# Work moved into TensorE's waits in a two-layer vision kernel, and a new order for its closing rounds

## Chip, cores and metric

The kernel runs on one core of a Trainium2 chip. The metric is the device time of one execution in microseconds, from the first instruction to the last. Five engines work in parallel, each through its own queue in order: TensorE (PE in the profile, its weight loads PEld), VectorE (DVE), ScalarE (ACT), GpSimd (POOL), and SyncE (SP), which issues the transfers. They wait for one another by semaphores.

## What is computed

The input is (2, 96, 256, 256) in float32, taken through two layers. Each layer is x + mixer(norm(x)), then t + FFN(norm(t)) for every pixel's 96 channels.

```python
# layer 0
x = x + window_attention(_ln_c(x))      # 8x8 windows, 12x12 keys (halo 2), 6 heads of 16, rel. positions
t = t + ffn(_ln_t(t), W1, b1, W2, b2)   # 96 -> 384 -> 96, relu, products in fp8 (5, 2), sums in fp16
# layer 1
x = x + cluster(_ln_c(x))               # features, 4 centres per head and fold, cosine, sigmoid, argmax,
                                        # aggregate to the centres, mix back, projection
t = t + ffn(_ln_t(t), ...)
```

In layer 1 the centres are means of the normalised pixels over quarters of a quadrant, so every similarity of a quadrant needs the whole quadrant, and the mix needs the sums over all similarities of the quadrant.

## The kernel before

The image is cut into N = 128 strips: 8 quadrants of 128x128 pixels, 16 strips of 8 rows each. A strip has 16 windows, handled as 8 tiles `p` of two. All stages of one step `n` of the pipeline are written into one in-order list for each engine. Step n does the attention of strip n; the normalisation, keys and queries of strip n+1 (`ahead`); the first FFN of strip n-1 (`b1`); the features and similarities of layer 1 for strip n-18 (`b`, LAG_B = 18); the mix of strip n-34 (`c1`, LAG_C = 34); the hidden part of the second FFN of strip n-35 (`c2`); and its output for n-36 (`c3`). So strips 35 to 127 have every stage. After strip 127 there are closing rounds, `drain`: 18 with features (`b`), 16 with only the mix and the second FFN, and two more.

The order is by hand. In `attend` TensorE goes for each tile through scores(p+1), inserted work, `flip(p, 0)` and `flip(p, 1)` (transposes of the shifted scores, L723 and L726, into the two banks `flipped`), `weigh(p-1)` (probabilities times values, L745 and L751), and more inserted work. ScalarE takes exponentials out of `flipped` (L1241, L1244), VectorE takes maxima (L1573) and subtracts them (L1577, L1581). scores(p+1) waits until VectorE has shifted tile p. The inserted work shares the PSUM banks: `work` (two banks), `fill`, which is the two banks of `flipped`, `misc`, and `pv`.

What the change touches, with the lines of the profile: `mean` (L607) of the next strip and its variances (L616, twelve small matmuls into `misc`); the first FFN's transposes `flip_z` (L917, copied to z8t by ScalarE at L1309), hidden tiles (L930), bias on VectorE (L1720), quantise on ScalarE (L1320), output (L940); `make_keys` (L643, stored at L1184); queries (L660, L663, stored at L1190); the second FFN's `flip_zc` (L999), hidden_c (L1009, copied at L1371, bias L1871, quantise L1377), output_c (L1017, copied at L1383, added at L1877 and L1881); `flip_sims` (L985, stored at L1360); `mix` (L992, added at L1836); `best_of`, the ranking (L1805 to L1824), and `gather` (L975). hidden(3) is the first of the second half and waits for the second z8t. In the closing rounds: feature transposes (L958, copied at L1342), features (L965), squares (L1349), comparison (L1775), sums (L1780), root steps (L1452 to L1476), z8c (L1864), cosine (L1796).

## Time and profile before

| | us |
|---|---|
| median of 3 runs | 8884.77 (8862.72 to 8898.8) |
| profiled execution | 8874.92, its span 8873.0 |
| busy in the span | PE 7728.7 (87%), PEld 6203.8 (70%), DVE 6895.1 (78%), ACT 4875.0 (55%), POOL 2496.1 (28%) |
| transfers | 501.76 MB, mean 57 GB/s |

A busy share is an average over strips and closing rounds, which have different limits. The last three of the 40 slices of the span (about 665 us) are closing rounds: there the granted clock of TensorE is 0.5 to 0.6 of full speed and no engine is full. "issue" as a releaser means that the profile shows nothing that the engine waited for.

### The profile page before, as it was taken

The numbers are of one execution on the slowest core, as the hardware profiler recorded it, in microseconds if no ns is written. First come the engines' busy times: TensorE is split into PE (matmuls) and PEld (weight loads), VectorE is DVE, ScalarE is ACT, GpSimd is POOL, SyncE is SP. The second block draws the span as 40 slices with busy tenths as digits, with TensorE's granted clock in tenths as the row PEclk, the third lists the DMA queues.
The fourth block names the chain that finished last, engine by engine and source line by source line (L and its number), as shares of the span: only waits on it lengthen the run. The fifth ranks groups of instructions, "written<-read, shape, count | busy, mean of one in ns | idle before, by whom it ended". The sixth has DMA issues, their size and how long they took to land.

```text
span 8873.0 us, 429305 instructions
## 1 busy us (share of the span) xinstructions
PE 7728.7 (87%) x172050; PEld 6203.8 (70%) x172050; DVE 6895.1 (78%) x22530; ACT 4875.0 (55%) x9750; POOL 2496.1 (28%) x4860
## 2 busy tenths in 40 slices
PE   6999999998999899988999889998998989997655
PEld 4777777777777777777777777776777777775433
DVE  3677777777888888888888778887888878887666
ACT  2444545545656565555656556555565556655445
POOL 1333333333332333333232322322333223322000
PEclk7899999999999999999999989999999999998556
DMA  2111111121222222222222212222222222221111
GB/s 58 41 43 43 45 45 50 51 52 50 64 59 64 57 62 58 61 61 57 62 59 62 57 54 62 59 62 58 61 58 63 57 56 64 61 62 50 59 55 60
DMA packets 193344, 501.76 MB, mean 57 GB/s; under 512 B 33508, under 2 KB 67108, under 8 KB 191468
## 3 DMA queue, kind: packets, MB, share of 16 engines
q1 hardware_dynamic: 191692, 476.75, 19.5%
q8 instruction: 1401, 22.95, 1.1%
q14 instruction: 251, 2.06, 0.1%
HBM read 228.84 MB, written 169.93 MB: 45 GB/s over the span
## 4 chain that ended last, share of the span: by engine, by line
PE 67%; DVE 15%; issue 8%; ACT 8%; DMA 1%; SPq 0%; ACTq 0%; DVEq 0%; POOL 0%; POOLq 0%
PE scores_x L701 11%; PE flipped L723 6%; PE bank L660 6%; PE pv L751 4%; DVE maxes L1573 4%; PE bank L663 3%; PE misc L616 3%; PE bank L965 3%; PE bank L671 3%; PE scores_x L643 3%; PE bank L607 3%; PE pv L745 3%; DVE shifted L1581 2%; PE bank L678 2%; PE flipped L992 2%
## 5 line engine op out<-in xcount | busy, mean ns | idle before, releaser
L2049 POOL TENSOR_TENSOR vrest<-vstage,vmask 96x384 f32<-96x384 f32 x512 | 437.2, 854 | 4643.4 <-ACT vstage L1202 4643.4
L1573 DVE TENSOR_REDUCE maxes<-scores_x 128x6 f32<-128x864 f32 x1024 | 1077.6, 1052 | 757.3 <-PE scores_x L701 754.0
L701 PE MATMUL scores_x<-keys,queries 64*64 64x144 f32 x24576 | 1060.7, 304 | 102.4 <-DVE shifted L1581 67.0
L701 PEld LDWEIGHTS scores_x<-keys,queries 64*64 64x64 f32 x24576 | 777.5, 140 | 337.5 <-issue 295.7
L663 PE MATMUL bank<-xn,wq 97*32 97x64 f32 x24576 | 919.9, 224 | 88.5 <-issue 86.7
L660 PE MATMUL bank<-xt,wq 97*32 97x64 f32 x24576 | 899.0, 224 | 88.3 <-issue 84.0
L1581 DVE TENSOR_TENSOR shifted<-scores_x,maxes 128x768 f32<-128x768 f32 x1024 | 970.1, 947 | 0.0
L660 PEld LDWEIGHTS bank<-xt,wq 97*32 97x32 f32 x24576 | 758.7, 112 | 268.9 <-issue 203.8
L723 PE MATMUL flipped<-ident,shifted 128*128 128x128 f32 x6144 | 891.6, 284 | 0.2 <-ACT vstage L1202 0.2
L663 PEld LDWEIGHTS bank<-xn,wq 97*32 97x32 f32 x24576 | 773.2, 110 | 108.7 <-issue 108.1
L1241 ACT ACTIVATE probs<-flipped 128x384 f32<-128x384 f32 x1024 | 498.7, 487 | 600.2 <-PE flipped L723 599.7
L1190 ACT ACTIVATE queries<-bank 128x512 f32<-128x512 f32 x768 | 456.2, 594 | 659.6 <-PE bank L663 658.9
L723 PEld LDWEIGHTS flipped<-ident,shifted 128*128 128x128 f32 x6144 | 741.0, 149 | 80.5 <-issue 48.2
L2062 POOL TENSOR_SCALAR xn<-x,mr 128x96 f32<-128x96 f32 x1024 | 689.9, 686 | 51.0 <-DVE mr L1476 33.1
L751 PE MATMUL pv<-vmain,probs 128*32 128x17 f32 x49152 | 633.6, 188 | 0.0
L1244 ACT ACTIVATE probs<-flipped 128x512 f32<-128x512 f32 x1024 | 612.2, 598 | 26.7 <-PE flipped L726 26.7
L751 PEld LDWEIGHTS pv<-vmain,probs 128*32 128x32 f32 x49152 | 624.2, 114 | 0.1
L2031 POOL COPY win_xn<-xn 97x144 f32<-97x144 f32 x2048 | 539.1, 310 | 0.0
L2022 POOL COPY xt<-xn 97x512 f32<-97x512 f32 x256 | 291.1, 1168 | 869.4 <-DVE xn L1541 755.7
L1371 ACT ACTIVATE h16c<-flipped 128x512 f16<-128x512 f32 x768 | 423.0, 593 | 181.0 <-PE flipped L1009 181.0
L1377 ACT ACTIVATE h8c<-h16c 128x512 fp8e5<-128x512 f16 x768 | 451.8, 627 | 17.7 <-DVE h16c L1871 13.5
L1314 ACT ACTIVATE h<-flipped 128x512 f16<-128x512 f32 x768 | 427.8, 595 | 48.3 <-PE flipped L930 39.1
(196 smaller groups left out, 17204.1 us busy)
## 6 DMA issues: line engine op xcount, KB each, us to landing
keys<-kst SPq DMA_DIRECT2D x768, 99.0 KB
x_in<-x_dram SPq DMA_DIRECT2D x130, 396.0 KB
xn_kept<-xn SPq DMA_DIRECT2D x128, 388.0 KB, 2.5
later<-xn_kept SPq DMA_DIRECT2D x128, 388.0 KB, 3.4
x_tok<-tok_dram SPq DMA_DIRECT2D x128, 384.0 KB, 3.1
x_kept<-x SPq DMA_DIRECT2D x128, 384.0 KB, 2.3
later<-x_kept SPq DMA_DIRECT2D x128, 384.0 KB, 3.7
out_dram<-later SPq DMA_DIRECT2D x128, 384.0 KB, 2.4
```

Of the source, the lines that this page charges most:

```text
L660: mm(dst[64 * e:64 * e + 32, :, :, j], wq[0:PROW, p * WS + j, 2 * g + e, :], xt[0:PROW, p, j, :, :], start=True, stop=True, skip_group_che ...
L663: last = mm(dst[64 * e + 32:64 * e + 64, :, j, :], wq[0:PROW, 2 * WS + j, 2 * g + e, :], rows[:, j], start=True, stop=True, skip_group_che ...
L701: last = mm(score[e][64 * j:64 * j + 64, g * NKEY:(g + 1) * NKEY], queries[64 * e:64 * e + 64, g, w, :], keys[64 * e:64 * e + 64, g, :, WS ...
L723: last = nc.tensor.transpose(flipped[:, e, g * 128:(g + 1) * 128], shifted[:, p % 2, e * NG + g, :], ident[:, :])
L751: last = mm(pv[tok_, at + i * VC:at + (i + 1) * VC], probs[:, p % 2, i, tok_], vmain[:, 2 * p + part // 2, i, :], start=False, stop=True, ...
L1190: run(queries[:, g, p:NW:2, :], work[i % 2][:, :].rearrange("p (w t) -> p w t", t=64), ACT.Copy).then_inc(q_stored.sem, 1)
L1241: run(probs[:, p % 2, 0:NG, :].rearrange("p i n -> p (i n)"), flipped[:, 0, 0:NG * 128], ACT.Exp).then_inc(exp_ready.sem, 1)
L1244: run(probs[:, p % 2, NG:NH + 1, :].rearrange("p i n -> p (i n)"), flipped[:, 1, :], ACT.Exp).then_inc(exp_ready.sem, 1)
L1573: V.tensor_reduce(maxes[:, p % 2, :, :], sc, AX.X, ALU.max).then_inc(max_ready.sem, 1)
L1581: V.tensor_tensor(shifted[:, p % 2, :, :].rearrange("p (e g) k -> p e g k", e=2), sc[:, :, :, 0:MAIN], maxes[:, p % 2, :, :, None].to_broa ...
L2031: last = P.tensor_copy(win_xn[:, w, :].rearrange("p (a b) -> p a b", b=KW), xn[0:PROW, :, WS * w:WS * w + KW])
L2062: last = P.tensor_scalar(xn2[:, t, 0:C], x2[:, t, :], mr[:, t, 0:1], mr[:, t, 1:2], ALU.subtract, ALU.mult)
```

## The change

In the strips with attention:
- TensorE: mean 1 goes from before the transposes of tile 0 to behind them. Variances 0 and 1 go from tile 3 to the end of tile 2, between hidden tiles 2 and 3 of the first FFN; only variance 2 stays in tile 3. For that, `flip_z` of the second half writes the second `fill` bank instead of `misc`, and hidden(3) waits for z8t. `make_keys` 0 and 1 go in front of the wait for the exponentials of tile 7 and hidden_c 4 and 5.
- ScalarE: in tile 4 the quantises 4 and 5 go in front of the copy of the similarities; keys 0 and 1 are stored before the hidden_c copies 4 and 5.
- VectorE: the ranking goes between the first and the second mix.

In the closing rounds:
- TensorE: similarities and features go in front of the transposes of the second FFN, whose six hidden tiles then follow in one run.
- VectorE: the two roots of a round (8 columns for the second FFN, 32 for the features) become one of 40. The ranking goes between hidden_c 2 and 3. It no longer adds the outputs.
- GpSimd adds the outputs in all closing rounds: two additions for each half.

```diff
@@ -317,7 +317,7 @@
         c_bn = signal("c_bn", 2, LAG_C + 1)
-        newton_z = signal("newton_z", 8, N)
+        newton_z = signal("newton_z", 8, N + LAG_B)
         rstd_z = signal("rstd_z", 1, LAG_C + 1)
@@ -608,8 +608,10 @@
             def variance(n, c, on=None):
-                if c == 0 and on and on.b1:
-                    pe.wait_ge(zt_ready.sem, zt_ready.at(n - 2, 2))
+                if c == 0 and on and on.b:
+                    pe.wait_ge(ft_ready.sem, ft_ready.at(n - 1, 2))
+                elif c == 0 and on and on.b1:
+                    pe.wait_ge(zt_ready.sem, zt_ready.at(n - 2, 1))
                 pe.wait_ge(squared.sem, squared.at(n, c + 1))
@@ -798,7 +800,6 @@
                         mean(n + 1, 0)
-                        mean(n + 1, 1)
                     if p == 1 and ahead:
@@ -808,8 +809,7 @@
                     if p == 3 and ahead:
-                        for c in range(3):
-                            variance(n + 1, c, on)
+                        variance(n + 1, 2, on)
                     if p == 4:
@@ -839,6 +839,8 @@
                     if p == 0:
+                        if ahead:
+                            mean(n + 1, 1)
                         if on.c3:
@@ -848,9 +850,13 @@
                     if p == 2 and b1:
-                        if on.b:
-                            pe.wait_ge(ft_ready.sem, ft_ready.at(n, 2))
+                        pe.wait_ge(exp_ready.sem, exp_ready.at(n, 6))
+                        pe.wait_ge(h_evac.sem, h_evac.at(n - 1, 2))
                         flip_z(n - 1, 1)
+                        hidden(n - 1, 2)
+                    if p == 2 and ahead:
+                        variance(n + 1, 0, on)
+                        variance(n + 1, 1, on)
                     if p == 3 and on.c2:
@@ -865,7 +871,8 @@
                         pe.wait_ge(exp_ready.sem, exp_ready.at(n, 2 * p + 2))
-                        hidden(n - 1, 2 * p - 2)
+                        if p != 2:
+                            hidden(n - 1, 2 * p - 2)
                         hidden(n - 1, 2 * p - 1)
@@ -873,13 +880,13 @@
                         output(n - 1, 1)
+                    if p == 7 and ahead:
+                        make_keys(n + 1, 0)
+                        make_keys(n + 1, 1)
                     if on.c2 and p in (5, 6, 7):
...
                         hidden_c(n, 2 * p - 9)
-                if ahead:
-                    make_keys(n + 1, 0)
-                    make_keys(n + 1, 1)
                 weigh(TILES - 1)
@@ -913,8 +920,9 @@
                 pe.sem_inc(gate, 1)
+                dst = fill[1] if u else misc
                 for j in range(4):
-                    last = mm(misc[0:C, j * 128:(j + 1) * 128], z8[:, 4 * u + j, :], ident8[:, :],
+                    last = mm(dst[0:C, j * 128:(j + 1) * 128], z8[:, 4 * u + j, :], ident8[:, :],
                               start=True, stop=True)
@@ -922,6 +930,8 @@
                     pe.wait_ge(zt_ready.sem, zt_ready.at(f, u + 1))
+                if i == 3:
+                    pe.wait_ge(zt_ready.sem, zt_ready.at(f, 2))
                 if i >= 2:
@@ -1026,6 +1036,7 @@
                     flip_z(n, 1)
+                    pe.wait_ge(zt_ready.sem, zt_ready.at(n, 2))
                     for i in range(2 * NK):
@@ -1045,26 +1056,22 @@
                     flip_features(n, 1, k % 2)
+                if on.c1:
+                    flip_sims(n, on)
                 if on.c2:
                     pe.wait_ge(mixed.sem, mixed.at(n, 0))
+                if on.b:
+                    features(n, 0)
+                    features(n, 1)
+                    pe.wait_ge(fsq_ready.sem, fsq_ready.at(n, 2))
+                    pe.wait_ge(dots_ready.sem, dots_ready.at(n, 2))
+                if on.c2:
                     flip_zc(n, 0)
...
                         pe.wait_ge(yc_evac.sem, yc_evac.at(n, 2))
-                    for i in range(NK):
+                    for i in range(2 * NK):
                         hidden_c(n, i)
-                if on.c1:
-                    flip_sims(n, on)
-                if on.b:
-                    pe.wait_ge(zct_ready.sem, zct_ready.at(n, 2))
-                    features(n, 0)
-                    features(n, 1)
-                if on.c2:
-                    for i in range(NK, 2 * NK):
-                        hidden_c(n, i)
-                if on.b:
-                    pe.wait_ge(fsq_ready.sem, fsq_ready.at(n, 2))
-                    pe.wait_ge(dots_ready.sem, dots_ready.at(n, 2))
                 if on.c1:
@@ -1271,13 +1278,17 @@
                     if p == 4:
+                        if b1:
+                            quantise(n - 1, 4)
+                            quantise(n - 1, 5)
                         if on.c1:
...
                         if b1:
-                            quantise(n - 1, 4)
-                            quantise(n - 1, 5)
                             output(n - 1, 0)
                             output(n - 1, 1)
+                    if p == 7 and ahead:
+                        store_keys(n + 1, 0)
+                        store_keys(n + 1, 1)
                     if on.c2 and p in (5, 6, 7):
@@ -1287,8 +1298,6 @@
                 if ahead:
-                    store_keys(n + 1, 0)
-                    store_keys(n + 1, 1)
                     store_queries(n + 1, 0)
@@ -1306,7 +1315,7 @@
                 act.sem_inc(gate, 1)
-                run(z8t[:, u, :], misc[0:C, :], ACT.Copy, saturate=False).then_inc(zt_ready.sem, 1)
+                run(z8t[:, u, :], (fill[1] if u else misc)[0:C, :], ACT.Copy, saturate=False).then_inc(zt_ready.sem, 1)
@@ -1395,25 +1404,22 @@
                     flip_features(n, 1)
-                if on.c2:
-                    store_zc(n, 0)
-                    store_zc(n, 1)
-                    for i in range(NK):
-                        hidden_c(n, i)
-                        if i >= 1:
-                            quantise_c(n, i - 1)
                 if on.c1:
...
                 if on.c2:
-                    for i in range(NK, 2 * NK):
-                        hidden_c(n, i)
-                        quantise_c(n, i - 1)
-                    quantise_c(n, 2 * NK - 1)
+                    store_zc(n, 0)
+                    store_zc(n, 1)
                 if on.b:
                     similarity(n)
+                if on.c2:
+                    for i in range(2 * NK):
+                        hidden_c(n, i)
+                        if i >= 1:
+                            quantise_c(n, i - 1)
+                    quantise_c(n, 2 * NK - 1)
@@ -1666,9 +1672,10 @@
                     mix(n, 0, par, fill)
-                    mix(n, 1, par, fill)
                 if on.b:
                     best_of(n)
+                if on.c1:
+                    mix(n, 1, par, fill)
                 residual(1)
@@ -1884,20 +1891,28 @@
                     stats_c(n, 1 - par)
-                    rsqrt_c(n)
-                    normalise_c(n, 1 - par)
-                if on.c3:
-                    output_c(n, 0, par)
-                    output_c(n, 1, par)
-                if on.c2:
-                    for i in range(NK):
-                        hidden_c(n, i)
                 if on.b:
...
                     squares_sum(n, 1)
+                    dve.wait_ge(c_bn.sem, c_bn.at(n, 2))
+                    V.tensor_scalar(rs_b_chain[0][:, 32:32 + TILES], mv_z[:, :, 1], 1e-5, None, ALU.add)
                     lengths(n)
+                    rsqrt(rs_b_chain, n, 128, 32 + TILES, newton_d, 0,
+                          [(0, TILES * E1, rs_b_chain[3][:, 0:32], newton_n),
+                           (32, TILES, rs_c_chain[3][:, :], rstd_z)])
+                elif on.c2:
+                    rsqrt_c(n)
+                if on.c2:
+                    normalise_c(n, 1 - par)
+                if on.b:
+                    cosine(n)
+                if on.c2:
+                    for i in range(NK):
+                        hidden_c(n, i)
+                if on.b:
+                    best_of(n)
                 if on.c2:
@@ -1905,9 +1920,6 @@
                 if on.b:
-                    lone_root(n)
-                    cosine(n)
-                    best_of(n)
                     add_gathered(n)
@@ -2087,6 +2099,17 @@
+            def output_c(n, u, par):
+                pool.wait_ge(yc_evac.sem, yc_evac.at(n, u + 1))
+                pool.sem_inc(gate, 1)
+                P.tensor_tensor(y16c[:, u, :, :], y16c[:, u, :, :],
+                                b2q[1][:, None, :].to_broadcast([128, 4, C]), ALU.add
+                                ).then_inc(yc_biased.sem, 1)
+                pool.wait_ge(yc_biased.sem, yc_biased.at(n, u + 1))
+                pool.sem_inc(gate, 1)
+                P.tensor_tensor(xc[par][:, 4 * u:4 * u + 4, :], xc[par][:, 4 * u:4 * u + 4, :],
+                                y16c[:, u, :, :], ALU.add).then_inc(xc_ready.sem, 1)
+
             def strip(n, on, column=0):
@@ -2117,6 +2140,10 @@
             normalise_stream(N - 1)
+            with pool.Fori(0, (LAG_C + 2) // 2) as s:
+                for par in range(2):
+                    for u in range(2):
+                        output_c(2 * s + (N + par), u, par)
```

## Rows read from the trace of the kernel before

**Rows 1.** Stretches, one strip and some closing rounds: length, busy PE, PEld, DVE, ACT, POOL, clock, DMA
```profile
5031.88:5095.15 63.27, 56.22 (x1346) 45.55 (x1343) 52.41 (x171) 37.50 (x76) 19.50 (x38) 1.00 0.22 61
...
8250.00:8500.00 250.00, 151.98 (x840) 103.87 (x840) 165.37 (x680) 115.10 (x220) 0.00 (x0) 0.55 0.18 58
```

**Rows 2.** What TensorE waited for, 4000 to 7000 us: total us, times, longest
```profile
PE flipped L940 <- ACT h L1320: 44.8, 46, 1.0
PE flipped L1017 <- ACT probs L1244: 36.9, 47, 1.0
PE bank L663 <- issue: 35.3, 48, 1.6
...
PE flipped L930 <- ACT z8t L1309: 29.1, 46, 0.6
PE flipped L1009 <- ACT probs L1244: 29.0, 46, 0.6
...
PE pv L975 <- DVE simw L1824: 20.5, 33, 1.0
```

**Rows 3.** Timeline of one strip, tiles 0 to 5: start, us, engine, line, operation
```profile
5037.82 1.35 PE L607 MATMUL bank<-x_in,mean_w 96*97 96x352 f32 x4
...
5053.99 2.04 PE L616 MATMUL misc<-mean_w,kst 96*88 96x1 f32 x24
...
5054.13 1.06 DVE L1573 TENSOR_REDUCE maxes<-scores_x 128x6 f32<-128x864 f32 x1 [0.31 <-PE scores_x L701]
...
5059.69 1.06 DVE L1573 TENSOR_REDUCE maxes<-scores_x 128x6 f32<-128x864 f32 x1 [0.21 <-PE scores_x L701]
...
5061.91 1.27 DVE L1720 TENSOR_SCALAR h<-h,b1q 128x512 f16<-128x512 f16 x2
...
5062.18 0.84 POOL L2049 TENSOR_TENSOR vrest<-vstage,vmask 96x384 f32<-96x384 f32 x1 [15.78 <-ACT vstage L1202]
...
5063.64 1.14 ACT L1320 ACTIVATE h<-h 128x512 fp8e5<-128x512 f16 x2
...
5064.92 0.67 PE L940 MATMUL flipped<-w2q,h 128*128 128x96 fp8e5 x12 [1.01 <-ACT h L1320]
```

**Rows 4.** Timeline, the end of that strip and of the next, by engine
```profile
5078.65 1.35 PE L643 MATMUL scores_x<-xn,wk 97*96 97x352 f32 x4
...
5090.72 0.55 DVE L1836 TENSOR_TENSOR later<-later,flipped 128x384 f32<-128x384 f32 x1 [2.91 <-PE flipped L992]
...
5094.21 0.29 DVE L1824 TENSOR_TENSOR simw<-winners,sims 128x128 f32<-128x128 f32 x1 [0.20 <-DVE winners L1819]
...
5094.19 0.59 ACT L1190 ACTIVATE queries<-bank 128x512 f32<-128x512 f32 x1
```

**Rows 5.** Timeline of one closing round with features
```profile
8330.38 0.88 PE L975 MATMUL pv<-later,simw 128*32 128x97 f32 x16 [6.62 <-DVE simw L1824]
...
8335.63 0.60 ACT L1342 ACTIVATE later<-misc 97x512 f32<-97x512 f32 x1 [0.77 <-PE misc L958]
...
8335.74 2.00 DVE L1864 TENSOR_SCALAR z8c<-later,mv_z,rz 128x96 fp8e5<-128x96 f32 x8 [0.24 <-DVE rz L1476]
...
8338.90 1.07 ACT L1371 ACTIVATE h16c<-flipped 128x512 f16<-128x512 f32 x2
...
8340.43 3.59 PE L965 MATMUL bank<-wfa,later 97*128 97x112 f32 x16
```

**Rows 6.** Timeline of one of the last closing rounds, without features
```profile
8641.22 1.38 DVE L1843 BATCH_NORM_STATS2 bn_z<-later 128x6 f32<-128x96 f32 x8
...
8645.44 2.01 DVE L1864 TENSOR_SCALAR z8c<-later,mv_z,rz 128x96 fp8e5<-128x96 f32 x8 [0.24 <-DVE rz L1476]
...
8651.56 0.37 ACT L1360 ACTIVATE simw_t<-misc 128x256 f32<-128x256 f32 x1
```

**Rows 7.** One line each, 3300 to 8000 us: duration in ns, minimum/median/maximum
```profile
L1471 DVE SCALAR_TENSOR_TENSOR rn<-rn x77: 157/192/850, 3320.9 to 7973.4; 128x44 f32<-128x44 f32 x73, 96x4 f32<-96x4 f32 x4
...
L2068 POOL TENSOR_TENSOR xn_half<-xn x73: 869/875/879, 3300.0 to 7953.5; 128x388 f32<-128x388 f32 x73
```

## The prediction

> **What bounds the kernel now.** I read, in this order, the busy time of stretches, the waits of TensorE, and the timeline of one strip and of the closing rounds. A strip in full swing lasts 63.27 us; TensorE is busy for 56.22 of them, VectorE for 52.41, ScalarE for 37.50, GpSimd for 19.50 [rows 1]. So TensorE sets the strip's length, but VectorE is only 4 us behind, and what TensorE gains in one place counts only if VectorE can follow there. In the closing rounds no engine is full: in 250 us TensorE is busy for 151.98 and VectorE for 165.37, at a granted clock of 0.55 [rows 1]. There the round is a chain of latencies through three engines.
>
> The waits of TensorE over 47 strips show where its missing time lies [rows 2]. Per wait: 44.8/46 = 0.97 us in front of the second FFN output for ScalarE's last quantise; 36.9/47 = 0.79 in front of the layer 1 output (L1017) for the exponentials of tile 0; 29.1/46 = 0.63 in front of hidden tile 3 for z8t; 29.0/46 = 0.63 in front of hidden_c 4 for the exponentials of tile 7; 20.5/33 = 0.62 before the gather, in two strips of three, so about 0.4 a strip. Sum: 3.4 us a strip. The "issue" stops inside the queries (35.3/48 = 0.74 us each for L663) have no releaser in this profile, and the change does not touch them.
>
> **The full strips, part by part.** None of the edits adds or removes an instruction here; each moves work into one of those waits.
>
> Mean of chunk 1. Four passes for two chunks take 1.35 us, so one chunk about 0.6 [rows 3]. It leaves the place before the first transpose of tile 0, the transpose and the exponentials start 0.6 earlier, and it fills most of the 0.79. Gain 0.6, if nothing later binds.
>
> Variances 0 and 1. All three cost 2.04 us [rows 3], two of them 1.3. They fill the 0.63 before hidden tile 3, but are longer than it: scores of tile 4 go out 1.3 - 0.63 = 0.7 later than they would. With the 0.6 of the mean taken off, they come where they were, within 0.1. Two thirds of the variances no longer stand in front of the transpose of tile 3, so TensorE is 1.3 earlier from there on. VectorE is not: its maxima of tile 4 start at 5054.13 after 0.31 idle, those of tile 5 at 5059.69 after only 0.21 idle [rows 3], so between them it can give back 0.2. Through tile 5 VectorE decides, and TensorE's 1.3 us is so far a lead without effect.
>
> Quantise before the copy of the similarities. VectorE biases hidden tiles 4 and 5 from 5061.91 to 5063.18, where the second is held up by a GpSimd product (5062.18 to 5063.02) [rows 3]. ScalarE now quantises them from 5063.64 to 5064.78, and the second output starts at 5064.92 [rows 3]. With the copy moved behind, and ScalarE's exponentials earlier by TensorE's lead, the first quantise can start right behind the first bias (about 5062.4 to 5062.6) and the second ends at 5063.7 to 5063.9. The output starts at 5064.0: gain 0.9. This is where the lead of the two edits above and this one are cashed, 0.9 of 0.6 + 0.63 + 0.97 = 2.2; the rest goes to VectorE's pace.
>
> Keys 0 and 1. The two chunks (1.35 us with the drain of the last one [rows 4]) go in front of the wait for tile 7's exponentials and fill its 0.63. ScalarE stores them before the hidden_c copies instead of after, which leaves the length of its queue as it is. Gain 0.6.
>
> Ranking before the second mix. VectorE stood idle for 2.91 us until the second mix was ready, and only then ranked, from about 5091.2 to 5094.5 [rows 4]. Ranking is 3.3 us; placed into the idle time it ends 2.9 us earlier and the gather's wait goes. What is late next is the last copy of queries on ScalarE, ending at 5094.78 [rows 4], 0.9 us after TensorE's last query and needed by the next scores: the gather (0.54) hides only part of it. Gain 0.25. The second mix and the residual come after the ranking, still before TensorE's end.
>
> Sum: 0.9 + 0.6 + 0.25 = 1.75 a strip. I take 0.2 off because the "issue" stops sit in the stretch that now starts earlier and may grow: 1.55. The bounds are 0.5 (only the keys) and 3.4 (every wait closed). Such strips are those with all stages, 35 to 127: 93, so 144 us; bounds 46 and 316.
>
> The 34 earlier strips with a first FFN have no output_c and no hidden_c, so there the mean and the keys win nothing. Only the variances' 0.63 is left, against scores of tile 4 being 0.7 later for VectorE. I take 0.2 x 34 = 7 us, bounds -20 and +21.
>
> **Closing rounds with features (18).** One lasts 25.0 us. Now: gather at 8330.38, statistics, their own root, z8c at 8335.74 (5.4 later), the first hidden copy at 8338.90, the features between the hidden tiles at 8340.43 for 3.59, mix, then a second root (eight steps, about 1.8 us), cosine, exponential and the ranking (3.3), and the gather [rows 5]. After: the root waits for the features. Both feature transposes are copied at 8335.63 + 0.60, 5.85 after the gather [rows 5]; similarities 0.45, features 3.6, the squares 0.7, the comparison 0.2, the sums 1.0, the two small steps 0.4, the one root 2.1: z8c starts at 14.3 instead of 5.4. From there, without the 3.59 of features in the middle: hidden copy at 18.1 (3.16 as now, plus the similarity's 0.5), third bias at 20.8, ranking until 24.1, and only then biases 3 to 5. The last quantise ends near 27.0, against the gather at 24.9. The next round's second output waits for it (27.1 to 28.0), and its transposes follow. They now start 2.65 after the gather; 28.05 - 2.65 = 25.4. So the round is 0.4 longer: the second root (1.8) and the ranking come off the end, and the wait for the features is put in front. 18 x 0.4 = +7 us. The single steps have half a microsecond of doubt each, 1.5 a round: bounds -20 and +34.
>
> **Rounds without features (16, and the last ones).** The similarity copy (0.37, at 8651.56 among the hidden copies [rows 6]) leaves ScalarE's chain: -0.4. The output adds leave VectorE, where they stood in the shadow of the z8ct copies and cost nothing; GpSimd has four of them. No row has a 16-bit add on GpSimd; the nearest is a 32-bit sum of 388 elements, 875 ns [rows 7]. So they last about 4 x 0.9 = 3.6, roughly from 8642.3 to 8646.4 in the round of rows 6, over the root between the statistics (8641.22) and z8c (8645.44) [rows 6]. This is the cover that is missing: a root step of VectorE that overlaps a GpSimd product takes up to 850 ns instead of a median of 192 [rows 7], and the bias of [rows 3] took 1.27 for two for the same reason. If all steps in that span give way, z8c is 2.1 later; if GpSimd gives way, nothing. I take 1.2. In sum +0.8 x 17 = +14 us, bounds -7 and +29. The store of the outputs starts 2 to 3 us earlier, but only the odd round waits for it.
>
> The Trainium skill, "SBUF — State Buffer", section "SBUF: two separate sides", says that VectorE and GpSimd share a port pair under an exclusive lock held for a whole instruction, which a VectorE operation with two SBUF inputs needs. Row and rule agree on the kind of the wait; by the rule alone each two-input step meets a GpSimd add and the upper bound of +29 would hold. In the rounds with features the adds fall on the statistics, which have one input, and by row and rule cost nothing.
>
> **Sum.** -144 - 7 + 7 + 14 = -130 us. Against the profiled execution's own 8874.9 that gives 8745; the median of the runs is 8884.8, 10 above it, and I predict 8755 for the median.
>
> **Rivals.** *The gain is given back.* VectorE, 4 us behind TensorE [rows 1], keeps the pace past tile 5 as well, or the "issue" stops grow by what the keys gain. For it: 0.21 idle before tile 5 [rows 3]. Against it: VectorE is idle 2.91 at the end. A strip then gains 0.7: -65 - 0 + 21, near 8840.
> *All waits close.* VectorE follows since its own held-up operations shift away from GpSimd's. A strip gains 2.6, 93 x 2.6 = 242, the closings 0: near 8640. Against it is the same 0.21.
> *Slower.* The 1.3 us of variances in front of hidden tile 3 delay the scores of tile 4, and VectorE, which waits for those scores already (0.31 [rows 3]), is 0.7 later in each of 127 strips. It decides if scores 4 end later than now and VectorE is the bound from there to the end of the strip: +89, less 34 (0.37 in 93 strips) that the end of the strip would still give, so 8940. Against it: TensorE, not VectorE, has the longer busy time.
> *The port.* The strips gain as forecast, the closings cost their upper bounds, +34 + 29 instead of +21: near 8797. The lock that the page on SBUF describes would give this case.
>
> **How the numbers follow.** Forecast 0.52 (8755, its own range 8700 to 8800), given back 0.17, all waits close 0.13, slower 0.08, the port 0.10. For 8 in 10 the range reaches into the second and third: 8655 to 8850. What a measurement can tell from no change is 0.5%, 44 us. Faster: the forecast, all waits close, the port, and half of given back, which is 0.52 + 0.13 + 0.10 + 0.09 = 0.84, less 0.04 for a forecast that fails by its lower bounds: 0.80. Same 0.12, slower 0.08.
>
> **What the next profile would show.** Right: a strip of 61.5 to 62; no wait of L1017 over 0.3; no wait of hidden tile 3 for z8t; the second output's wait at 0.5 or less; no wait of hidden_c for the exponentials; the gather's wait gone and a short one of the scores for the last queries; maxima of tile 5 with no idle time before them. In the closings one root of 40 columns, rounds near 25.4, then 15 to 16.5 with root steps of over 0.5 us beside GpSimd's adds. Wrong: scores 4 later than 22 us after scores 0 with VectorE idle before its maxima; stops inside the queries well over 1.5 us a strip; or closing rounds over 27 us.

## The result, and the profile after

The changed kernel takes 8495.31 us in the median of 4 runs (8466.25 to 8505.01), beside 8887.02 (8862.72 to 8898.8) for the kernel before on the same chip: ratio 0.9557, 95% interval 0.9526 to 0.9588. Forecast were 8755 us and a range from 8655: the direction is right, the time lies outside. Three times the forecast gain came.

The profiled execution has a span of 8464.2 us. Stretches: one strip, a piece of the closing rounds with features, and VectorE's tile 4 of that strip. Columns as in [rows 1].

```profile
4225.86:4285.45 59.59, 55.72 (x1344) 45.29 (x1345) 51.87 (x172) 37.65 (x76) 19.54 (x38) 1.00 0.24 65
7770.00:8020.00 250.00, 142.78 (x934) 86.77 (x934) 145.97 (x635) 123.58 (x239) 39.64 (x44) 0.70 0.19 61
4246.79:4252.05 5.26, 5.19 (x114) 4.37 (x115) 4.89 (x16) 4.22 (x10) 0.00 (x0) 1.00 0.15 59
```

The waits of TensorE from 4000 to 7000 us (total, times, longest), against [rows 2]:

```profile
PE scores_x L703 <- ACT queries L1197: 51.5, 46, 1.2
PE flipped L950 <- ACT h L1329: 32.6, 42, 1.5
PE bank L665 <- issue: 21.5, 42, 1.3
PE scores_x L703 <- DVE shifted L1587: 20.6, 44, 0.7
PE bank L662 <- issue: 17.6, 34, 1.3
...
PE flipped L1027 <- ACT probs L1251: 9.2, 49, 0.3
```

The layer 1 output's wait fell from 0.79 to 9.2/49 = 0.19; those for z8t, of hidden_c for the exponentials, and of the gather are gone. The second output of the first FFN (L950; the second FFN output of the prediction) still waits 32.6/42 = 0.78, where 0.5 or less was forecast. New is the wait of the first scores for the last query copy, 51.5/46 = 1.12, which the prediction named as next and thought short.

So far this reads like the forecast with a little more. The rest shows only when all strips are measured. I took the starts of VectorE's maxima of each tile, over strips 36 to 127, and worked out the means (us):

| | tile 3 to 4 | 4 to 5 | 5 to 6 | 7 to next 0 | strip |
|---|---|---|---|---|---|
| before | 5.17 | 6.93 | 6.86 | 24.01 | 64.26 |
| after | 5.00 | 5.28 | 5.66 | 23.21 | 60.47 |

The other stretches differ by 0.04 or less. A full strip lost 3.8 us where 1.55 was forecast; over these 92 strips 349 us, the 35 before them 46, and what comes behind the last strip's maxima went from 770 to 757. That is 408 of the 409 us between the spans. The largest piece is where the prediction said VectorE allows 0.2: from tile 4 to tile 5. Its intervals there are of three kinds. Of 91 strips before, 27 took 5.6 us, 38 took 6.9 and 26 took 8.5 (medians of the kinds); after, all 91 took about 5.26. The prediction had read a strip of the first kind.

A strip of the third kind, of the kernel before, first the stretch from maxima 4 to maxima 5 and then its timeline:

```profile
4538.11:4546.58 8.47, 8.47 (x122) 7.04 (x123) 4.97 (x14) 4.27 (x10) 0.00 (x0) 0.60 0.06 20
```
```profile
4536.77 0.38 PE L930 MATMUL flipped<-z8t,w1q 96*128 96x512 fp8e5 x1 [0.64 <-ACT z8t L1309]
4537.08 0.97 PE L701 MATMUL scores_x<-keys,queries 64*64 64x144 f32 x24
4537.98 2.71 PE L616 MATMUL misc<-mean_w,kst 96*88 96x1 f32 x24
4540.54 1.52 PE L723 MATMUL flipped<-ident,shifted 128*128 128x128 f32 x6
...
4545.19 1.31 PE L701 MATMUL scores_x<-keys,queries 64*64 64x144 f32 x24
...
4546.58 1.06 DVE L1573 TENSOR_REDUCE maxes<-scores_x 128x6 f32<-128x864 f32 x1 [3.13 <-PE scores_x L701]
```

TensorE has a matmul under way for all 8.47 us, but at a granted clock of 0.60, which is a mix of its two levels that is mostly the lower (1.2 GHz). From the run of one-column variances (L616) on everything is slower: the six transposes take 1.52 us, the scores 1.31 instead of 0.97, and VectorE stands idle for 3.13 us. Of the 64 strips of the second and third kind, all 64 have a stretch at the lower level between these two maxima; of the 27 others 1 has. The strip of [rows 1] and [rows 3] had a clock of 1.00 and 0.21 of idle at the same place.

The clock record of that trace has the lower level from 4539.13 for 6.83 us: it begins 1.15 us into the run, which for that reason lasts 2.71 and not 2.04.

The same place after:

```profile
4243.80 0.39 PE L925 MATMUL flipped<-ident,z 128*96 128x128 fp8e5 x4
4244.03 0.38 PE L940 MATMUL flipped<-z8t,w1q 96*128 96x512 fp8e5 x1
4244.25 1.34 PE L618 MATMUL misc<-mean_w,kst 96*88 96x1 f32 x16
4245.45 0.38 PE L940 MATMUL flipped<-z8t,w1q 96*128 96x512 fp8e5 x1
4245.75 0.97 PE L703 MATMUL scores_x<-keys,queries 64*64 64x144 f32 x24
4246.65 0.79 PE L618 MATMUL misc<-mean_w,kst 96*88 96x1 f32 x8
4247.30 0.85 PE L725 MATMUL flipped<-ident,shifted 128*128 128x128 f32 x6
```

The run is cut in two by a hidden tile and the scores, and the transposes take 0.85. Variances 0 and 1 fill the wait for z8t: the scores of tile 4 start 3.94 us behind maxima 3, where they started 4.07 behind before, and the transposes of tile 3 start 1.5 us earlier (5.41 against 6.90, medians over strips 40 to 125).

Of the closing rounds, the one with features, from gather (8010.08) to gather (8032.28) (L985; L975 before):

```profile
8010.08 0.74 PE L985 MATMUL pv<-later,simw 128*32 128x97 f32 x16
...
8014.89 0.60 ACT L1351 ACTIVATE later<-misc 97x512 f32<-97x512 f32 x1 [0.77 <-PE misc L968]
...
8015.87 1.94 PE L975 MATMUL bank<-wfa,later 97*128 97x112 f32 x16
...
8021.98 2.01 DVE L1871 TENSOR_SCALAR z8c<-later,mv_z,rz 128x96 fp8e5<-128x96 f32 x8 [0.25 <-DVE rz L1482]
...
8025.76 1.06 ACT L1380 ACTIVATE h16c<-flipped 128x512 f16<-128x512 f32 x2
...
8032.28 0.88 PE L985 MATMUL pv<-later,simw 128*32 128x97 f32 x16
```

The features take 1.94 us and not the 3.59 of [rows 5]. z8c starts 11.9 behind the gather, 14.3 was forecast; the round is 22.2 long, 25.4 was forecast, 25.0 before. A round without features, VectorE's root and GpSimd's adds:

```profile
8289.96 1.38 DVE L1850 BATCH_NORM_STATS2 bn_z<-later 128x6 f32<-128x96 f32 x8
8291.08 0.91 POOL L2105 TENSOR_TENSOR y16c<-y16c,b2q 128x384 f16<-128x384 f16 x1 [12.80 <-ACT y16c L1392]
...
8292.17 0.94 POOL L2110 TENSOR_TENSOR later<-later,y16c 128x384 f32<-128x384 f32 x1 [0.18 <-POOL y16c L2105]
8292.37 0.76 DVE L1458 TENSOR_SCALAR rz<-rz 128x8 int32<-128x8 int32 x1
8293.07 0.90 POOL L2105 TENSOR_TENSOR y16c<-y16c,b2q 128x384 f16<-128x384 f16 x1
8293.17 0.83 DVE L1465 TENSOR_TENSOR rz<-rz 128x8 f32<-128x8 f32 x1
8294.03 0.17 DVE L1467 TENSOR_TENSOR rz<-rz 128x8 f32<-128x8 f32 x1
8294.15 0.91 POOL L2110 TENSOR_TENSOR later<-later,y16c 128x384 f32<-128x384 f32 x1 [0.18 <-POOL y16c L2105]
8294.23 0.85 DVE L1469 SCALAR_TENSOR_TENSOR rz<-rz 128x8 f32<-128x8 f32 x1
...
8306.75 1.38 DVE L1850 BATCH_NORM_STATS2 bn_z<-later 128x6 f32<-128x96 f32 x8
```

Three root steps of 0.17 us take 0.76 to 0.85, each until the GpSimd add beside it ends. From statistics to statistics (8289.96 to 8306.75) the round takes 16.8 us; it took 15.2. So the closing rounds gained in the first kind and lost in the second: from the last gather to the end it is 299 us, where it was 268, while the whole behind the last maxima got 13 shorter.

### The profile page after: what moved, and what is told of

The parts are those of the page before. It is cut to its first block, busy times and chain, and to the rows that moved or that the text cites. A ratio compares the mean times of both kernels' runs of the same rounds, so it can differ in the third digit from the quotient of the medians.

```text
span 8464.2 us, 429416 instructions
## 1 busy us (share of the span) xinstructions
PE 7468.5 (88%) x172050; PEld 6008.7 (71%) x172050; DVE 6788.1 (80%) x22260; ACT 4867.1 (58%) x9750; POOL 2630.1 (31%) x5004
## 3 DMA queue, kind: packets, MB, share of 16 engines
q14 instruction: 252, 2.06, 0.1%
## 4 chain that ended last, share of the span: by engine, by line
PE 59%; DVE 24%; issue 9%; ACT 5%; DMA 1%; DVEq 0%; SPq 0%; ACTq 0%; POOL 0%; POOLq 0%
PE scores_x L703 8%; DVE maxes L1579 6%; PE bank L662 6%; PE flipped L725 5%; PE bank L665 3%; PE pv L753 3%; PE scores_x L645 3%; DVE shifted L1587 3%; PE misc L782 3%; PE pv L747 2%; PE bank L673 2%; PE bank L975 2%; PE flipped L1019 2%; DVE z8c L1871 2%; PE flipped L1002 2%
## 5 line engine op out<-in xcount | busy, mean ns | idle before, releaser
L703 PE MATMUL scores_x<-keys,queries 64*64 64x144 f32 x24576 | 1033.5, 298 | 190.2 <-ACT queries L1197 102.2
L703 PEld LDWEIGHTS scores_x<-keys,queries 64*64 64x64 f32 x24576 | 752.0, 136 | 409.4 <-issue 375.3
L665 PE MATMUL bank<-xn,wq 97*32 97x64 f32 x24576 | 910.5, 224 | 76.6 <-issue 75.5
L725 PE MATMUL flipped<-ident,shifted 128*128 128x128 f32 x6144 | 858.1, 276 | 0.2 <-ACT vstage L1209 0.2
L665 PEld LDWEIGHTS bank<-xn,wq 97*32 97x32 f32 x24576 | 770.6, 110 | 87.2 <-issue 85.5
L725 PEld LDWEIGHTS flipped<-ident,shifted 128*128 128x128 f32 x6144 | 712.9, 144 | 80.4 <-issue 47.7
L753 PEld LDWEIGHTS pv<-vmain,probs 128*32 128x32 f32 x49152 | 603.8, 111 | 0.6 <-issue 0.6
L1878 DVE TENSOR_SCALAR h16c<-h16c,b1q 128x512 f16<-128x512 f16 x768 | 357.8, 497 | 160.6 <-ACT h16c L1380 156.0
```

The lines of the kernel that those rows point to most:

```text
L665: last = mm(dst[64 * e + 32:64 * e + 64, :, j, :], wq[0:PROW, 2 * WS + j, 2 * g + e, :], rows[:, j], start=True, stop=True, skip_group_che ...
L703: last = mm(score[e][64 * j:64 * j + 64, g * NKEY:(g + 1) * NKEY], queries[64 * e:64 * e + 64, g, w, :], keys[64 * e:64 * e + 64, g, :, WS ...
L725: last = nc.tensor.transpose(flipped[:, e, g * 128:(g + 1) * 128], shifted[:, p % 2, e * NG + g, :], ident[:, :])
L753: last = mm(pv[tok_, at + i * VC:at + (i + 1) * VC], probs[:, p % 2, i, tok_], vmain[:, 2 * p + part // 2, i, :], start=False, stop=True, ...
```

## The experiments

All times are medians of 4 runs (e1 and e13: 10). The ratio is to the kernel before, run beside it on the same chip, with its 95% interval. The stretches and the strip are means over strips 36 to 127 of the one profiled execution. "Clock" is the granted clock of the stretch 2200 to 7650 us of it; 0.96 in the kernel before are 68 stretches at the lower level, 410 us in all.

How far to trust the strip: the changed kernel, e18 (the same again), e12 and e4 (which differ behind the strips only) have 60.47, 60.50, 60.27 and 60.56 us. A difference of 0.3 between two executions can be chance.

### The run of variances: where it stands

**e1**: before, variance 2 alone moved in front of `weigh(2)`, behind the transposes of tile 3. Variances 0 and 1 stay in front of them.
```diff
-                        for c in range(3):
+                        for c in range(2):
                             variance(n + 1, c, on)
                     flip(p, 0)
                     flip(p, 1)
+                    if p == 3 and ahead:
+                        variance(n + 1, 2, on)
```
**e2**: after, all three variances in tile 3. **e3**: after, all three at the end of tile 2.
```diff
-                    if p == 2 and ahead:          # e2
-                        variance(n + 1, 0, on)
-                        variance(n + 1, 1, on)
                     if p == 3 and ahead:
-                        variance(n + 1, 2, on)
+                        for c in range(3):
+                            variance(n + 1, c, on)
```


> The kernel before, with one edit: variance 2 of the next strip goes behind the transposes of tile 3 instead of standing in one run with variances 0 and 1 in front of them. Clock theory: in the kernel before the run of twelve matmuls of one column (2.0 us) is followed in many strips by a stretch at the lower level of TensorE's granted clock (4923 to 4931 us: 0.61), which makes the way from the maxima of tile 4 to those of tile 5 last 6.9 us at the median and up to 8.5 instead of 5.6. With the run cut in two the clock stays, tile 4 to tile 5 is 5.6 in nearly all strips, and the kernel is 100 to 200 us shorter. Order theory: the gain of the change comes from the filled wait for z8t and the earlier transposes; this edit fills no wait, so the time is that of the kernel before within 20 us.

> The changed kernel with all three variances back in tile 3 in one run; every other edit stays, also the z8t transposes into the other bank. Clock theory: the stretches at the lower clock come back, tile 4 to tile 5 goes from 5.3 to about 6.9 at the median, the mean granted clock falls from 0.94 towards 0.915, and the kernel is 150 to 220 us longer than the changed one. Order theory: only the 0.63 us wait for z8t comes back, and VectorE absorbs a part: 30 to 60 us longer, with tile 4 to tile 5 under 6 us in most strips.

> The changed kernel with all three variances in one run at the end of tile 2, between hidden tiles 2 and 3, and none in tile 3. The wait for z8t is filled and the transposes of tile 3 are earlier still. Order theory: as fast as the changed kernel, within 30 us. Clock theory: the run is whole, so the lower clock follows it as before, only half a tile earlier: 100 to 220 us longer than the changed kernel.

| | time | ratio | tile 3 to 4 | 4 to 5 | 5 to 6 | 7 to 0 | strip | clock |
|---|---|---|---|---|---|---|---|---|
| e1 | 8844.8 | 0.9951 (0.9932 to 0.9970) | 5.16 | 6.50 | 6.86 | 24.05 | 63.84 | 0.97 |
| e2 | 8696.3 | 0.9773 (0.9739 to 0.9807) | 4.88 | 6.61 | 5.99 | 23.12 | 61.96 | 0.96 |
| e3 | 8604.2 | 0.9689 (0.9657 to 0.9721) | 5.74 | 5.24 | 5.76 | 23.31 | 61.48 | 0.97 |

e1 gave 41 us, less than half of what the clock theory wanted, and stands at the edge of what the prediction calls no change (0.5%): a run of eight still stands in front of the transposes, and 35 of 91 strips are still over 6 us. e2 loses 201 us to the changed kernel, as that theory expected and more than three times what the order could. In 62 of 91 strips maxima 5 are late, as before the change. e3 loses 109: at tile 4 to 5 nothing, but a whole run at the end of tile 2 delays the scores of tile 4 (5.74 against 5.00), and more low clock is left than the 0.99 of the changed kernel. The clock still falls there: 44 of 91 strips have the lower level beginning between tiles 3 and 5, against 12 in the changed kernel, and TensorE was busy for at least 4.8 of the 5 us before each of these. But no strip is over 6 us from maxima 4 to 5. So the place of the run also settles what a fall of the clock costs.

### The run of variances: how wide its matmuls are

Place and order speak in all three. To leave them as they are, each matmul got 32 columns instead of one. The same weights are loaded, the same number of matmuls runs; 32 equal copies of each mean are written, of which VectorE reads one.
```diff
-                    last = mm(misc[0:VT, t:t + 1], squares[c][:, j * VT:(j + 1) * VT],
-                              mean_w[:, 0:1], start=True, stop=True)
+                    last = mm(misc[0:VT, 32 * t:32 * t + 32], squares[c][:, j * VT:(j + 1) * VT],
+                              mean_w[:, 0:32], start=True, stop=True)
...
-                V.tensor_scalar(rs_b_chain[0][0:VT, 32:44], misc[0:VT, 0:12], 1e-6, None, ALU.add
+                V.tensor_scalar(rs_b_chain[0][0:VT, 32:44], misc[0:VT, 0:384:32], 1e-6, None, ALU.add
```
**e5** is e2 with that, **e9** the kernel before with that and nothing else.

> The changed kernel with all twelve variance matmuls in tile 3, as in the earlier run of that form (8,696 us), but each matmul 32 columns wide instead of one (32 equal copies of the mean of squares; VectorE reads every 32nd). The order of work, the weights loaded and the results are the same; the run itself can only get longer. Theory 'order' (the run is in the way in tile 3, whatever the clock): the same or slower, 8,690 to 8,740. Theory 'clock' (the granted clock falls to 1.2 GHz behind a run of one-column matmuls because the array has next to nothing to do in them): fewer stretches at 1.2 GHz than the 70 of the one-column form, and a time below 8,640; if all of them go, near 8,500. If the clock falls just as often with 32 columns, the width is not what matters, and the time is 8,690 or more.

> The kernel before, with nothing moved: only each variance matmul is 32 columns wide instead of one. Theory 'clock': most of the 410 to 437 us of stretches at 1.2 GHz between 2,200 us and the end of the strips go, and a full strip loses about the 1.5 us of tiles 4 and 5; 8,680 to 8,780. Theory 'order' (the gain of the change comes from where its steps stand): 8,870 to 8,900.

| | time | ratio | tile 3 to 4 | 4 to 5 | 5 to 6 | 7 to 0 | strip | clock |
|---|---|---|---|---|---|---|---|---|
| e5 | 8554.2 | 0.9637 (0.9612 to 0.9662) | 4.89 | 5.56 | 6.01 | 23.12 | 60.93 | 0.98 |
| e9 | 8730.5 | 0.9825 (0.9777 to 0.9873) | 5.17 | 5.76 | 6.88 | 24.05 | 63.13 | 0.98 |

Two pairs that differ in the width alone: 142 us and 144 us. In e9 10 of 91 strips are late at maxima 5 instead of 64, in e5 9 instead of 62. The same strip as above, in e9: maxima 4 to maxima 5, and its timeline.
```profile
4465.61:4471.23 5.62, 5.55 (x122) 4.71 (x123) 4.97 (x14) 3.33 (x8) 0.00 (x0) 1.00 0.10 34
```
```profile
4465.48 2.06 PE L616 MATMUL misc<-mean_w,kst 96*88 96x32 f32 x24
4467.38 0.85 PE L723 MATMUL flipped<-ident,shifted 128*128 128x128 f32 x6
...
4471.23 1.06 DVE L1573 TENSOR_REDUCE maxes<-scores_x 128x6 f32<-128x864 f32 x1 [0.28 <-PE scores_x L701]
```
The run lasts 2.06 us, as long as the 2.04 of [rows 3], though it does 32 times the columns, and the clock behind it is 1.00. So the clock is shown as the cause of the late maxima: it falls to 1.2 GHz in this run or behind it when its matmuls are one column wide, and mostly stays when they are 32. (In the kernel before, of 65 stretches at the lower level that begin between tiles 3 and 5, 32 begin in the run and 32 up to 1.4 us behind its end.)

The clock records also show where it still falls. The changed kernel has 23 stretches at the lower level from 2200 to 7650 us, 160 us in all. 12 of them (41 us) begin between tiles 3 and 5, by the variances; in e10 and e17, the changed strip with 32 columns, there is none. The other 11 (119 us) begin at the end of a strip, and e10 keeps 10 such (123 us). Nearly all of those stand beside idle time of TensorE: 1.1 us before the first scores, "issue" stops of 1.2 to 1.6, and above all one strip in every 16 (49, 65, 81, 97, 113), where the centres of a new quadrant leave TensorE idle for up to 4.8 us before L1095 and 3.1 before L1118.

The Trainium skill, "TensorE: Matmul & The Clock Gate", section "Part 1: The HAM clock gate (the "warmup" mystery)", names idle time of TensorE as what the clock falls after. By that rule alone the kernel before should have kept its clock in the row of 8.47 us above: from 4536 to 4546.58 TensorE was idle for 0.63 us in all, and e9 has as much before its run (29.7/47 in front of hidden tile 3) and keeps the clock. The measurement decides: a stretch full of matmul records ran mostly at the lower level. At the ends of strips 65, 81 and 97 the trace agrees with the Trainium skill: there, in e10, idle time of 4.1 to 4.8 us stands beside the fall.

### The other steps of the strip

**e6** keys 0 and 1 back behind tile 7; **e7** the copy of the similarities back in front of quantises 4 and 5; **e15** mean 1 back in front of the transposes; **e16** the ranking back behind the second mix; **e11** all four back at once, so that of the strip's changes only the variances and the step of `flip_z` are left. The main line of each:
```diff
-                    if p == 7 and ahead:      # e6, PE; ScalarE's stores likewise
-                        make_keys(n + 1, 0)
-                        make_keys(n + 1, 1)
...
+                        if on.c1:             # e7
+                            store_sims(n)
                         if b1:
                             quantise(n - 1, 4)
                             quantise(n - 1, 5)
-                        if on.c1:
-                            store_sims(n)
...
                         mean(n + 1, 0)        # e15
+                        mean(n + 1, 1)
...
-                if on.b:                      # e16
-                    best_of(n)
                 if on.c1:
                     mix(n, 1, par, fill)
+                if on.b:
+                    best_of(n)
```
**e13** is the kernel before with the step of `flip_z` alone (own bank for the second half, no wait for ft_ready, hidden(2) right behind it; the variances wait for ft_ready and zt_ready as in the change), **e14** the same with 32 columns.
```diff
-                        if on.b:
-                            pe.wait_ge(ft_ready.sem, ft_ready.at(n, 2))
+                        pe.wait_ge(exp_ready.sem, exp_ready.at(n, 6))
+                        pe.wait_ge(h_evac.sem, h_evac.at(n - 1, 2))
                         flip_z(n - 1, 1)
+                        hidden(n - 1, 2)
...
+                dst = fill[1] if u else misc
```


> The changed kernel, with keys 0 and 1 again behind tile 7 on TensorE and behind all the quantising on ScalarE. The prediction gave keys in front 0.6 us a strip: 60 to 80 us slower than the changed kernel (8,555 to 8,575). Rival: the new wait of the first scores for the last query copy (1.1 us a strip after the change) shows that the end of the strip is set by the queries, which the keys don't touch: within 15 us of 8,495.

> The changed kernel, with ScalarE's copy of the centres' distances again in front of the two quantisings of tile 4 (as before the change). The prediction let these, with the mean and the variances, give 0.9 us a strip together. If the order of ScalarE carries a third of it: 25 to 40 us slower (8,520 to 8,535). Rival: nearly all of the gain of tiles 4 and 5 is the clock, and this is within 10 us of 8,495.

> The changed kernel, with keys, quantising, ranking and the second mean all put back where they were; the variances in two parts, the flip of z8 with its own bank and the closing rounds stay. The prediction gave the moved steps other than the variances 0.25 (ranking) + 0.6 (keys) + some 0.4 (quantising, mean) us a strip: 100 to 120 us slower than the changed kernel, 8,595 to 8,615. Theory 'clock': the variances alone carry nearly everything, 8,495 to 8,530, since keys and quantising put back singly cost 7 and 5 us.

> The kernel before, with one step of the change alone: the second half of z8 is flipped into a PSUM bank of its own, no longer waits for the features' copy, and the hidden layer's third matmul comes right behind it. The variances stay in one run in tile 3. By the traces, the forms that have this step (5.96 to 6.08 us from the maxima of tile 5 to those of 6, 23.1 to 23.4 from tile 7 to the next strip) stand against those without it (6.86 to 6.93, and 24.0), whatever else they have: 1.2 to 1.6 us a strip, 110 to 150 us faster than the kernel before (8,725 to 8,775). Rival: these two stretches are shortened by the clock or by the closings' neighbours, and this step by itself is within 20 us of 8,885.

> The kernel before, with the flip of z8 as in the run above and the variance matmuls 32 columns wide, in one run in tile 3. If the two causes (the clock behind the run, 150 us; the flip's wait, 110 to 150 us) are independent, 8,580 to 8,640. If they are the same stall seen twice, it is no faster than the better of the two alone, 8,700 to 8,740.

> The changed kernel, with the second mean again right behind the first. Variances alone lost 62 us to the whole change, keys and quantising put back singly lost 7 and 5, so the mean and the ranking hold some 50 us or the parts work only together. In that run the maxima of tile 4 came 0.56 us later behind those of tile 3, which the mean could do (its centres are late for the squares): 20 to 50 us slower than the changed kernel, 8,515 to 8,545. Rival: within 10 us of 8,495.

> The changed kernel, with the ranking again behind the second mixing on VectorE. The prediction gave it 0.25 us a strip: 20 to 25 us slower, 8,515 to 8,520. Rival: VectorE's order there is covered, within 10 us of 8,495.

| | time | ratio | tile 3 to 4 | 4 to 5 | 5 to 6 | 7 to 0 | strip |
|---|---|---|---|---|---|---|---|
| e6 keys | 8502.0 | 0.9573 (0.9553 to 0.9593) | 4.97 | 5.28 | 5.67 | 23.48 | 60.82 |
| e7 quantise | 8500.6 | 0.9566 (0.9538 to 0.9593) | 4.99 | 5.27 | 5.96 | 23.09 | 60.66 |
| e15 mean | 8491.7 | 0.9596 (0.9551 to 0.9642) | 5.57 | 5.29 | 5.67 | 22.92 | 60.70 |
| e16 ranking | 8455.0 | 0.9540 (0.9502 to 0.9579) | 5.00 | 5.30 | 5.67 | 22.92 | 60.16 |
| e11 all four | 8557.4 | 0.9635 (0.9602 to 0.9668) | 5.56 | 5.32 | 6.08 | 23.36 | 61.79 |
| e13 flip_z | 8843.1 | 0.9968 (0.9945 to 0.9991) | 5.27 | 7.12 | 6.84 | 23.31 | 63.89 |
| e14 flip_z, wide | 8686.3 | 0.9811 (0.9758 to 0.9864) | 5.25 | 5.79 | 6.83 | 23.36 | 62.60 |

The waits of TensorE (4000 to 7000 us) show that the edits do what they say. In e6 the wait of hidden_c is back, in e16 the gather's wait is back and half of the wait for the last queries goes in exchange:
```profile
PE flipped L1019 <- ACT probs L1251: 30.6, 48, 0.6
```
```profile
PE scores_x L703 <- ACT queries L1197: 24.4, 39, 1.0
...
PE pv L985 <- DVE simw L1831: 17.1, 36, 1.0
```
But none of the four, put back alone, costs a time that this measurement can tell from no change. Put back together they cost 1.3 us a strip and a ratio of 0.9635 against 0.9557: singly their strips add up to 0.35 + 0.19 + 0.23 - 0.31 = 0.46, each of them near the 0.3 that can be chance.

e13 was my theory for what the clock leaves, drawn from the table: every fast form had the step. It fell. Alone it brings 0.3%, and tile 5 to 6 stays at 6.84. Two things take that stretch down, and they cover for each other. One is the place of the variances: 6.84 in e13, 6.08 in e11, which have the same flip. In e11 the scores of tile 5 end 1.02 us ahead of maxima 5, in e13 only 0.07 (medians). The other is the four steps: e2 has them with the whole run in tile 3, without that lead (0.07), and is at 5.99; the wait of the second output for the last quantise (L947 in e13, 45.9/46) is not among its waits. Either gives about 0.8, both together 1.2 (5.66). That is why e7 alone shows 0.3. The end of the strip, in contrast, does fall with `flip_z` alone (24.01 to 23.31), since the "issue" stops in the queries fall: L663's 35.3/48 of [rows 2] are L665's 12.9/28 in e13. Why they fall, the profile does not show.

One path through the runs takes the 3.79 us of the strip apart:

| from | to | edit in the strip | us a strip |
|---|---|---|---|
| before | e9 | 32 columns | 1.13 |
| e9 | e14 | `flip_z` | 0.53 |
| e14 | e5 | the four other steps | 1.67 |
| e5 | e10 | variances 0 and 1 in tile 2 | 0.74 |
| e10 | after | one column again | -0.28 |

The last row lies within what can be chance. The clock is 0.98 or 0.99 in e9, e14, e5 and e10, so it has little part in the rows between them, and there the four steps are worth about what the prediction gave the whole strip (1.55). (e5, e10 and the changed kernel have new closing rounds too; these lie behind the last strip.) In times: 144 us for the first row, 44 for the second, 132 for the third with the closing rounds.

### The closing rounds

**e12**: after, with the drain rounds of the kernel before. **e4**: after, but GpSimd adds the outputs in the rounds with features alone; in the others VectorE does, behind `normalise_c`.
```diff
                 if on.c2:
                     normalise_c(n, 1 - par)
+                if on.c3 and not on.b:
+                    output_c(n, 0, par)
+                    output_c(n, 1, par)
...
-            with pool.Fori(0, (LAG_C + 2) // 2) as s:
+            with pool.Fori(0, LAG_B // 2) as s:
```


> The changed kernel with the closing rounds of the kernel before (features behind the hidden layer, two roots, VectorE adds the outputs). The closings of the profiled executions are 765 us before and 752 after: 5 to 25 us slower than the changed kernel, 8,500 to 8,520. The prediction's own sum (the change makes the closings 21 us longer) would have it 21 us faster, near 8,475.

> The changed kernel, with GpSimd adding the outputs only in the closing rounds with features, and VectorE adding them again in those without, between z8c and the first bias. Port theory: in the changed kernel three root steps of VectorE last 0.77, 0.84 and 0.86 us instead of 0.18 beside GpSimd's adds, and a round without features lasts 16.7 us; now they last 0.18 again and the round about 14.8 (15.2 of the kernel before less the 0.4 of the similarity copy): 16 times 1.9, so 30 us less than the changed kernel. Rival: the round is longer because the six hidden tiles now stand in one run and its copies wait for one another; then it stays at 16 to 16.7 and the time is the same within 10 us.

e12: 8481.5 us, ratio 0.9557 (0.9523 to 0.9592), the same as the changed kernel; behind the last strip's maxima it takes 771 us, the changed kernel 757 and 756 in its two profiled executions. So the new order is worth 14 us in the traces, too little for the medians. e4: 8458.5 us, 0.9508 (0.9475 to 0.9541), and 722 us. So 35 us are shown in the trace; the medians, whose intervals overlap, have 37. Its root steps take 0.17 and its rounds without features 14.9:
```profile
8304.33 1.38 DVE L1850 BATCH_NORM_STATS2 bn_z<-later 128x6 f32<-128x96 f32 x8
8306.74 0.17 DVE L1458 TENSOR_SCALAR rz<-rz 128x8 int32<-128x8 int32 x1
8306.94 0.17 DVE L1465 TENSOR_TENSOR rz<-rz 128x8 f32<-128x8 f32 x1
...
8319.24 1.38 DVE L1850 BATCH_NORM_STATS2 bn_z<-later 128x6 f32<-128x96 f32 x8
```

### What is faster still

**e8**: e4 with the variances in three pieces, variance 1 behind hidden(3). **e10**: e4 with 32 columns. **e17**: e10 with the ranking back. **e18**: the changed kernel again.
```diff
                         variance(n + 1, 0, on)           # e8
-                        variance(n + 1, 1, on)
...
                         hidden(n - 1, 2 * p - 1)
+                    if p == 2 and ahead:
+                        variance(n + 1, 1, on)
```


> The version in which GpSimd adds outputs in rounds with features alone (8,458 us in its run), and the variances in three pieces of four matmuls: 0 behind tile 1's weighing, 1 behind the hidden layer's second matmul of that place, 2 in front of tile 3's transposes. Theory 'clock': the 23 stretches at 1.2 GHz that the changed kernel still has between 2,200 and 7,650 us (160 us, worth about 60 to 80 us in time) become fewer, and the time falls by 20 to 60 us, to 8,400 to 8,440. Rival: what is left of low clock comes from elsewhere than the variances, and the time is within 10 us of 8,458.

> The version with GpSimd's adds in rounds with features alone (8,458 us in its run), with the variance matmuls 32 columns wide. Theory 'clock': the 23 stretches at 1.2 GHz left in the strips become few, and the time is 8,400 to 8,440. Rival: these stretches have other causes than the variances (the three pieces of another run did not end them), and the 12 wider matmuls cost what they save: 8,450 to 8,480.

> The fastest version so far (GpSimd's adds in rounds with features alone, variance matmuls 32 columns wide; 8,401 us) with the ranking put back behind the second mixing. Put back alone in the changed kernel it gave 8,455 against 8,495 us, though the prediction had it cost 20 to 25. If the earlier ranking really delays the second mixing and so the last query copies: 8,360 to 8,390. Rival: that difference lies between two calls of runs, and this is within 12 us of 8,401.

> The changed kernel once more, unchanged, beside the run above: it shows how far two medians of one kernel lie apart between calls. Same as before: 8,480 to 8,510, and a ratio of 0.954 to 0.958.

| | time | ratio | strip |
|---|---|---|---|
| e8 | 8480.4 | 0.9562 (0.9537 to 0.9586) | 60.63 |
| e10 | 8400.9 | 0.9464 (0.9431 to 0.9496) | 60.19 |
| e17 | 8418.4 | 0.9456 (0.9412 to 0.9500) | 60.21 |
| e18 | 8481.2 | 0.9523 (0.9473 to 0.9573) | 60.50 |

e18 shows that two medians of one kernel, taken at different times, lie 14 us apart, so keys, quantising, mean and ranking are each nothing that can be told. e16 had 8455 and made me ask whether the earlier ranking costs time; e17 does not bear that out (8418 against 8401). Three pieces bring nothing (e8). 32 columns on top of e4 bring 58 us between the medians (e10); the intervals of the ratios overlap (0.9475 to 0.9541 and 0.9431 to 0.9496), and the strip shows 0.37 us, 34 in all. e10 is the fastest version: 94 us below the changed kernel, or 80 below e18.

## Why the prediction was wrong

*The step that failed*: "VectorE is not: its maxima of tile 4 start at 5054.13 after 0.31 idle, those of tile 5 at 5059.69 after only 0.21 idle [rows 3], so between them it can give back 0.2. Through tile 5 VectorE decides, and TensorE's 1.3 us is so far a lead without effect." The rows are right, for a strip at full clock: there the interval went from 5.6 to 5.26. But in 64 of 91 strips it was 6.9 or 8.5, and TensorE at the lower clock decided. Forecast for tiles 4 to 6 were 0.9 us, measured 1.65 + 1.20 = 2.85 a strip. Two causes stand in place of that step: the clock in tile 4 to 5, and the lead, which does have an effect, in tile 5 to 6.

- *The clock*, missing from the sum. Width alone gives 142 and 144 us (e5 against e2, e9 against before). The strip that I read, 63.27 us, is 1 us shorter than the mean of 64.26; I had not laid it beside the others.
- *Variances and the wait for z8t.* The mechanism was right: they fill the 0.63 and the scores of tile 4 come no later. The size was not: TensorE's lead of 1.3 us was called "without effect". The stretch from tile 5 to 6, which it opens, lost 0.76 (e11 against e13) before the quantising adds anything, and the whole run in tile 3 costs 0.74 a strip against the split one when both have 32 columns (e5, e10).
- *Quantise before the copy.* It was to cash 0.9 together with the lead; behind the lead it brings 0.3 of tile 5 to 6 (e7), without the lead the four steps bring 0.85 there (e2 against e13), about the 0.9 forecast. The forecast took the two together for 0.9 of which VectorE would allow no more; together they gave 1.20 there (6.86 to 5.66), and the output's wait stayed at 0.78 instead of closing.
- *Mean.* Put back, its wait for the exponentials returns (0.78) and tile 3 to 4 is 0.57 longer, since the variances that came forward need the room. The end gives 0.3 back, and the time shows nothing (e15).
- *Keys*, 0.6 forecast, 0.35 a strip in the trace, 7 us in time (e6), hardly more than chance. *Ranking*, 0.25 forecast, nothing: gather's wait and queries' wait change places (e16). The prediction named that exchange and priced it too low.
- *"Issue" stops*, 0.2 of loss forecast. The prediction lets them grow; L663's 35.3/48 = 0.74 us became 21.5/42 = 0.51, and the end of the strip gained 0.80 as against the 0.85 - 0.2 of the sum. Near, but from a step that had no term: `flip_z` alone gives 0.7 of it (e13).
- *Early strips*, 7 us forecast, 46 measured in this pair of executions; the other three with the same strips (e18, e12, e4) give 33, 49 and 12. The run of variances has a part: e9 alone gives 38, and its time at the lower level up to there is 300 us instead of 403.
- *Rounds with features*, +0.4 forecast, -2.8 measured. The features stood at the 3.59 us of [rows 5], and z8c came 2.4 earlier than forecast; 1.65 of that is the features at 1.94. The granted clock of such a stretch is 0.70 and was 0.55. The sum had its bounds at -20 and +34; up to the last gather the closing rounds gained 45. e12 shows the price of the whole order of the closing rounds, 14 us gained instead of 21 lost.
- *Rounds without features*, +0.8 forecast, +1.6 measured, within the step's own bound of 1.7 (in all 31 us behind the last gather; the sum had +14, its bound +29). Each GpSimd add lasts 0.91 to 0.94 us in 16 bits and in 32, as taken from [rows 7]. Three steps gave way. e4 takes the adds away and the steps are 0.17 again: shown.

Of the rivals, "all waits close" with 8640 pointed the right way, with the wrong mechanism (VectorE's idle time, not the clock) and still 145 us short. The one-in-two forecast and the bounds of the strip (0.5 to 3.4 us) came from one strip and from waits alone; the measured 3.8 lies outside, since slow matmuls are busy time and stand in no list of waits.

What stays open: why `flip_z` shortens the "issue" stops; why the run of one-column matmuls lowers the clock in two strips of three and not in all; and how the 1.3 to 1.7 us of the four steps are shared among them, since each alone is too small to be told.

## What to carry to other kernels

Before a price is read from one strip, lay the same interval out over all of them: three kinds of 5.6, 6.9 and 8.5 us under a mean of 6.9 are a cause of their own. Do not add up two edits that shorten the same stretch: each may be worth all of it alone, and little behind the other. Read the granted clock of short stretches, between two marks of another engine, and not of whole strips: a TensorE that is busy at half clock looks like work. Where tiny matmuls run in a row in front of work that is urgent, cut the run, or make its matmuls wider at the same duration; that one edit was worth 144 us on the kernel before.
